# Moving VectorE's gate product two instructions later in a Mamba stage spread over four engines

## What is computed

```
x = x + _L0_conv_ref(_gn(x), ...)      # routed mixture of four 3x3 convolutions, three steps
x = x + _L1_conv_ref(_gn(x), ...)      # Mamba over rows, then Mamba over columns
```

```
xz = einsum('bld,ed->ble', x, in_w);  xi, z = split(xz)
xc = silu(conv4(xi) + conv_b)
dt, Bm, Cm = split(einsum('ble,fe->blf', xc, xproj_w))
dt = softplus(dt @ dt_w + dt_b);  A = -exp(A_log)
h  = exp(dt*A) * h + dt * Bm * xc          # the scan, for each of the 16 states
y  = sum_s(h * Cm) + xc * D
out = (y * silu(z)) @ out_w                 # y * silu(z) is the gate product
```

## Time and profile before

| | |
|---|---|
| median of three runs | 4038.09 us |
| the profiled execution | 4032.97 us |
| its span | 4031.2 us |
| DVE busy | 3748.4 us, 93% |
| PE busy | 3668.5 us, 91% |
| POOL busy | 3275.0 us, 81% |
| ACT busy | 2935.2 us, 73% |
| first and last gate product start | 814.2 and 4025.7 us |

### The profile page before, as it was taken

One profiled execution on the slowest core, in us unless ns is written; L12 is line 12 of the kernel. 1 busy time (PEld: TensorE's weight loads), 2 busy tenths in 40 slices (PEclk: granted clock), 3 DMA queues, 4 the chain that ended last, 5 costly groups with the idle time before them and its releaser, 6 DMA issues. The chain is left out here.

```text
span 4031.2 us, 34432 instructions
## 1 busy us (share of the span) xinstructions
PE 3668.5 (91%) x8780; PEld 1522.4 (38%) x8780; DVE 3748.4 (93%) x3418; ACT 2935.2 (73%) x4425; POOL 3275.0 (81%) x1542
## 2 busy tenths in 40 slices
PE   4999999699999999999999999999999999999998
PEld 2444444233333333333333333333333333333333
DVE  5687786599999999999999999999999999999998
ACT  3454544487887888878877887888878888887885
POOL 1121221399999999999999999999999999999998
PEclk9999999799999999999999999999999999999999
DMA  3133313588888888888888988888888888888886
GB/s 100 37 91 82 110 43 100 196 340 324 358 353 334 345 348 350 350 345 337 344 350 342 346 339 348 342 347 353 341 346 349 346 350 344 347 348 342 350 341 259
DMA packets 203157, 1181.06 MB, mean 293 GB/s; under 512 B 30960, under 2 KB 31760, under 8 KB 68816
## 3 DMA queue, kind: packets, MB, share of 16 engines
q1 hardware_dynamic: 202960, 1178.87, 76.2%
HBM read 1144.03 MB, written 34.73 MB: 292 GB/s over the span
## 5 line engine op out<-in xcount | busy, mean ns | idle before, releaser
L1363 POOL TENSOR_TENSOR read<-state,bc_all 128x1024 f32<-128x1024 f32 x1024 | 2399.9, 2361 | 109.8 <-DVE state L1420 80.6
L1420 DVE TENSOR_TENSOR_SCAN state<-decays,p_drive 128x1024 f32<-128x1024 f32 x1024 | 2298.2, 2274 | 59.5 <-ACT decays L1298 23.7
L1147 PE MATMUL p_y<-read,ident 128*128 128x512 f32 x4096 | 1927.0, 603 | 11.2 <-POOL read L1363 10.8
L1298 ACT ACTIVATE decays<-dt,wa 128x496 f32<-128x496 f32 x2048 | 1336.8, 703 | 126.8 <-DVE state L1420 124.4
L1147 PEld LDWEIGHTS p_y<-read,ident 128*128 128x128 f32 x4096 | 767.3, 191 | 992.2 <-issue 840.9
L1407 DVE TENSOR_TENSOR p_drive<-bc_all,p_dtx 128x1024 f32<-128x1024 f32 x768 | 906.3, 1210 | 0.0
L1380 POOL TENSOR_TENSOR pool_drive<-dtx,bc_all 128x1024 f32<-128x1024 f32 x256 | 602.8, 2354 | 10.6 <-DMA bc_all<-bc_scratch 10.5
L663 POOL TENSOR_TENSOR pad<-map_all,xc 128x512 f32<-128x512 f32 x96 | 135.7, 1444 | 547.1 <-DMA map_all<-map_scratch 434.1
L1306 ACT COPY p_drive<-pool_drive 128x1024 f32<-128x1024 f32 x256 | 260.8, 1019 | 272.3 <-DVE state L1420 272.3
L1143 PE MATMUL p_y<-xconv,d_diag 128*128 128x512 f32 x256 | 146.2, 653 | 205.9 <-DVE gated L1430 205.9
L501 PE MATMUL p_conv<-pad,wm 128*128 128x512 f32 x576 | 267.4, 600 | 1.7 <-issue 1.7
(11 more groups left out here) (166 smaller groups left out, 3158.8 us busy)
## 6 DMA issues: line engine op xcount, KB each, us to landing
bc_all<-bc_scratch SPq DMA_DIRECT2D x1024, 1024.0 KB, 7.1
map_all<-map_scratch SPq DMA_DIRECT2D x48, 512.0 KB, 5.8
norm_rows<-xn SPq DMA_DIRECT2D x32, 280.0 KB, 6.0
norm_in<-norm_rows SPq DMA_DIRECT2D x64, 140.0 KB, 6.4
norm_in<-norm_rows SPq DMA_DIRECT2D x64, 139.8 KB, 7.4
fresh<-in_x SPq DMA_DIRECT2D x32, 256.0 KB, 6.6
x<-in_x SPq DMA_DIRECT2D x32, 256.0 KB, 3.6
mid_x<-x SPq DMA_DIRECT2D x32, 256.0 KB, 6.2
```

The costliest lines, as they stand in the source:

```text
L1147: nc.tensor.matmul(p_y[:], ident[:], read[:, s % DEEP, :], start=False, stop=(s == N - 1)).then_inc(y_added, 1)
L1298: nc.scalar.activation(decays[:, s % DEEP, :].rearrange("p (q t) -> p q t", t=SIDE)[:, :, 1:], dt[b][:, :, 1:], ACT.Exp, scale=wa[m][:, s: ...
L1363: nc.gpsimd.tensor_tensor(read[:, s % DEEP:s % DEEP + 2, :], state[:, s % DEEP:s % DEEP + 2, :], bc_all[:, s:s + 2, 1, :], ALU.mult).then_ ...
L1420: nc.vector.tensor_tensor_scan(state[:, at:at + 2, :].rearrange("p s n -> p (s n)"), decays[:, at:at + 2, :].rearrange("p s n -> p (s n)") ...
```

## The change

In the first half of each of VectorE's slots (pairs 0 to 3), the gate product of the unit before is issued after the third scan and the fourth drive product, and no longer between the second scan and the third. Nothing is added or removed, and no other engine's program changes.

```
@@ -1436,10 +1436,10 @@
                     make_drives(u, p + 1)
                     make_drives(u, p + 2)
                     scan_pair(u, p + 1)
+                    scan_pair(u, p + 2)
+                    make_drives(u, p + 3)
                     if half == 0 and before:
                         apply_gate(u - 1, 1 - b, before)
-                    scan_pair(u, p + 2)
-                    make_drives(u, p + 3)
                     scan_pair(u, p + 3)
```

## The result

The changed kernel takes 4709.53 us (median of 4 runs, 4705.78 to 4711.04) against 4036.96 us before (median of 4): ratio 1.1664, 95% interval 1.1644 to 1.1684. It is 17% slower, where 13% was forecast, and lies 19.5 us above the range's upper end of 4690 us.

The account below looks back on a forecast made before the run. A loop from the gate product through TensorE and ScalarE back to VectorE, which set the pace, would bind: 4032.97 + 344 (loop) + 200 (clock) = 4577, plus 5.1 to the median, 4582 us; range 4380 to 4690.

Parts of the forecast that it names:

- The loop: Gate product, TensorE from L1143, ScalarE's soft step and move, VectorE's next first scan, gate product; binds every slot, +344 us.
- Leg 2: Mean time from ScalarE's soft_step 0 (L1259) to TensorE's next L1143; forecast parts 2.86 + 9.97 + 0.72 us.
- The slack of 0.75 us: Time before VectorE's first scan between ScalarE's move being handed over and the scan starting; the gate product starts 3.33 us later.
- VectorE still sets the pace: Rival, chance 0.02: VectorE remains the bound and the gate product fills a 22 us handover, giving 4016 us.
- no change: Rival, chance 0.03: VectorE's 99% stays the bound, only its instructions' places differ, 4038 us.
- The handover of 0.17 us at the fourth drive: VectorE's wait between fourth drive product and the scan reading it, filled by the gate product; possible 22 us gain, taken as 0.
- TensorE's clock: Idle 4.5 us before L1143 lowers TensorE's clock once a slot, 1.60 us each: +200 us.
- double fall: Two clock falls' worth in one TensorE slot, bound 3.20 us; in half the slots 4682 us, in all 4782.
- the clock costing more: Rival, chance 0.13: TensorE's clock falls overlap or come twice in many slots, 4682 to 4782 us.
- TensorE or ScalarE making up a part: Rival, chance 0.08: some instruction between L1143 and L1259 waits for something else and absorbs delay, 4100 to 4380 us.
- leg 1: Mean time from TensorE's L1143 to ScalarE's soft_step 0 (L1259); forecast read 14.23 us in the first slot.
- What was costed at nothing: Possible lateness of GpSimd's work and reads, ScalarE's B and C row copies and broadcasts, and the sixteenth state: 0 us.

Follow-up runs that it names:

- late_warm4: The changed kernel plus four extra matmuls on constants in front of L1143 in every slot, keeping TensorE at work: 4373.72 us, ratio 1.0823.
- late_act_first: The changed kernel with ScalarE's move of the next unit's first drive and its dtx copy put before copy_rows and soft_step 0: 4065.35 us, ratio 1.0061.
- late_two_scans: The changed kernel with the gate product moved behind the fourth scan too, without extra matmuls: 4936.09 us, ratio 1.2222.

## Why the prediction was right or wrong

- **The loop**: right. Leg 2 was worked out as 13.55 us and is 13.54. Slots in which the scan waits: 125. At full clock (late_warm4) the loss is 337 us against 344 on record. The two experiments that move the gate product by other distances lie on the same line.
- **The slack of 0.75 us**: right for the slot that it was read from. Over all slots it is smaller: the loop at full clock would take 14.49 + 13.54 - 3.33 = 24.70 us, 0.5 us under VectorE's pace of 25.19. The sum doesn't use it, since it adds up the loop slot by slot. The slack ruled out that VectorE still sets the pace, and it is why 99% busy was no protection. The Trainium skill's rule of the highest occupancy ("Perfetto Trace Analysis", "Identifying the Most-Contended Engine") would have given no change. Here the busiest engine was bound by a loop with 3% of a slot in reserve.
- **The handover of 0.17 us at the fourth drive**: it was there (2444.12 - 2443.00 = 1.12 to the gate product) and worth nothing, as taken, since VectorE waited in every slot. In late_act_first, where it nearly doesn't, one slot less its 0.31 us wait takes 25.10 us against 25.19, about half of the 0.17. No run isolates it.
- **TensorE's clock**: the step that failed. It read: "I take one fall a slot, since the two rows of long idle nearest to it both fell: 125 x 1.60 = **+200 us**". The runs show 4709.5 - 4373.7 = 336 us, 2.7 us a slot. That every slot falls was right; what a fall costs was mis-sized. The 1.60 us is the price of a low clock that lasts 3.4 us, all of it on work, after 1.91 us idle. After 4.48 us idle it lasts 6.8 us, of which 1.1 fall into the idle time and 5.8 on work at half speed: 2.8 us in the slot shown. The bound I had, 3.20, did hold it; the range stopped at half of the slots with a double fall, where 121 of the 125 lost 2.5 us or more. With the measured size the sum is 4033 + 344 + 336 = 4713 for the profiled execution, which took 4708.6.
- **Two readings behind that step** were weak too. The 1.60 compares a slot of one kind with another's `project_out`; against the same place in the body (L1143 to L1161 in 3.54 us) the fall cost 5.23 - 3.54 = 1.69. And the rows of long idle were a choice: of the 28 slots before the change with 1.90 or 1.91 us idle, 9 fell and 19 didn't. So "both fell" was no evidence for one fall in every slot. That all 125 did fall after 4.48 us was luck as far as those rows go.
- **The rivals**: the clock costing more had 0.13 and is what happened. TensorE or ScalarE making up a part had 0.08 and did not occur: leg 1 at full clock is 14.49 us, where the prediction's four slots average 14.51.
- **What was costed at nothing**: right for the loop. POOL's wait for the scan grows from 80.6 to 627.6 us because VectorE comes later, and PE's waits for POOL's reads are 5.1 us in all. One queue did get late: VectorE waits for ScalarE's decays 92 times where it waited twice, some 0.4 us each, about 10 us behind the gate product. Leg 2 doesn't contain that place and stays at 13.54.
- **What would show it**: VectorE's busy share in the stage 82% (85 said), wait for L1306 of 647.5 us (300 to 550 said), slots of 30.7 us (27.8 to 31).

## What to carry to other kernels

An engine that is 99% busy can still be one short slack away from a loop through the other engines. Before moving an instruction later, name the engine that its result releases, follow what is queued behind there until the chain comes back, and subtract: the slack decides, not the busy share. On TensorE, a longer idle time costs a second time through the clock, and the price has to come from a row with an idle time as long, or be bounded. Count also the rows with the same idle time in which nothing happened. Matmuls that compute nothing, put into the pause, can be a quick experiment that parts the two costs.

## What the runs showed of the hardware

- The clock's mean cost per slot against TensorE's idle time in front of L1143 (time over the twin at full clock, by 125 slots): 0 at 1.04 us, 0.77 at 2.76 us, (4462.5 - 4232.7) / 125 = 1.84 at 3.35 us, 2.69 at 4.48 us, 2.10 at 6.85 us. These are means: at 2.76 us most slots lost nothing and the others about 1.7 us. It is smaller at 6.85 us because more of the low clock falls into the idle time, as the granted clock of two slots shows; no run isolates it.
- In the granted clock a fall lasted 3.4 us in the kernel before and 6.8 us in the changed kernel and in `late_two_scans`. The loss in the four slots looked at is half of the part that falls on work, within 0.05 us.
- In the changed kernel the slots settle into a pattern: L1143 to L1143 takes 30.49, 31.06, 30.95 and 30.37 us, and the same four values recur body after body from 2629 to 2967 us to within 0.01 us. Before, slots with a fall came singly.
- In the kernel before, of the slots of units 1 to 126, 9 of the 28 with 1.90 or 1.91 us idle were followed by a low clock and none of the 98 with less. One 0.86 us matmul in the pause ended all the falls.
